# Writing out the three middle batches of a looped attention as straight programs on every engine

## The chip, the cores and the metric

The kernel runs on one core of a Trainium2 chip. The metric is the device time of one launch in microseconds, given as the median of three runs. All traces are of one profiled execution on that core.

## The reference

Input `x` has 4 batches of 256 tokens with 256 features. Three layers follow each other, each behind a layer norm without weights:

```python
x = x + 0.5 * ffn(layernorm(x), router_weight, w_in, w_out, bias)
x = x + attn(layernorm(x), w_q, w_k, w_v, w_o, b_o)
x = x + 0.5 * ffn(layernorm(x), router_weight, w_in, w_out, bias)
```

`ffn` is a mixture of 8 experts, of which each token uses the best two: `silu(a) * b @ w_out.T` with `a, b` the halves of `h = x @ w_in.T`, weighted by a softmax over the two router logits. `attn` is causal attention with 16 heads of 16 features: `q @ k.T / sqrt(256)`, softmax, times `v`, and a projection with `w_o` and a bias. All is in float32.

## The kernel before

TensorE (PE), VectorE (DVE), ScalarE (ACT), GpSimd (POOL) and the queue of SyncE each run a program of their own, and they meet only in semaphores. Products of float32 are taken with a high and a low part, so that most products are three matmuls. The order of the work on each engine is written out by hand.

The first and the last layer, `ffn(0)` and `ffn(1)`, go through 23 blocks of 128 gathered tokens. Seven of them are written out, the next fourteen lie in a loop on a register, the last two are written out again.

The attention, which is what the change touches, is a sweep over batches. `step(b, old, new)` issues eight steps `s` for batch `b`. In the steps 0 and 1 the pairs of heads 6 and 7 of the batch before (`old`) are scored, in the steps 2 to 7 the pairs 0 to 5 of the new batch; a pair goes through the engines with a lag of one step for each stage:

- PE, in every step: `scores` with the tail (the second 128 queries against 256 keys: three matmuls of 512 columns at L1553, a mask at L1554), `turn_probs` (six transposes at L1564, of the pair two steps back), `scores` with the head (three of 256 columns and a mask), `weigh` (18 small matmuls at L1579 to L1581, of the pair three steps back). The steps 0 and 3 also have a `chunk` of queries and keys (eight matmuls at L1520), step 6 has `turn_context` (L1593), step 7 begins with `project_out` (L1600).
- DVE: the maxima of the tail (L1174) and of the head (L1178), the low half of the turned probabilities (`low`, L1187, two for each pair); at the start of step 5 `add_up`, which sums the context of the old batch (L1195) and inverts the row sums (L1197); at the end of step 7 `add_attention` (L1202).
- ACT: the exponentials of tail and head (L792, L800), the high half of the turned probabilities (`high`, L810, two), two copies for each chunk (L778, L779), and in step 6 the copy of the turned context (L818).
- POOL: `mask_keys`, four multiplications (L607) that make `k_head` for the next tail; in step 6 also `divide` (L381).

Four waits set the order around step 5. `weigh` in step 5 overwrites the banks 5 and 6, and waits for both sums of `add_up` (`ctx_summed`). `turn_probs` waits until `low` has read the banks 3 and 4 (`pT_lo_ready`). `project_out` waits for the copy at L818 (`ctxT_ready`). The `chunk` of step 0 waits for `add_attention` of the batch before (`attn_added`), since both use bank 7.

`sweep` is called once by each of PE, DVE, ACT and POOL. It issues `step(0, False, True)` and `step(4, True, False)` as straight code and the batches 1 to 3 in `Fori`, a loop of the engine's sequencer, with `b` in a register. In the loop each wait compares a semaphore with a value computed from `b`, and operands such as `v[:, bass.ds(b * 2 + kt, 1), h, :]` in `weigh`, `xnT[:, k, bass.ds(b * SEQ, SEQ)]` in `chunk` and `row_sum[:, bass.ds(batch, 1), ...]` in the exponentials get their address from a register.

Of the kernel before, what the change touches and what calls it, by code (L numbers as in the profile page):

```python
# [23 lines left out]
BATCH, SEQ, D = 4, 256, 256  # L24
# [55 lines left out]
def build(nc, x_in, wq_in, wk_in, wv_in, wo_in, bo_in, wr_in, win_in, wout_in, bias_in, out):  # L80
    with ExitStack() as ctx:
# [283 lines left out]
        def sweep(eng, step):  # L365

            step(0, False, True)
            with eng.Fori(1, BATCH) as b:
                step(b, True, True)
            step(BATCH, True, False)  # L370

# [92 lines left out]
        def _(pool):  # L464
# [146 lines left out]
            def step(b, old, new):  # L611
                for s in steps_of(new):
# [4 lines left out]
                    if not old and s == BIAS_STEP:  # L617
                        add_bias(1, bo, TPAIRS - 2, 2)

            sweep(pool, step)  # L620
            inverse_root(2, 0, TPAIRS - 1)
            inverse_root(2, TPAIRS - 1)
# [4 lines left out]
        def _(act):  # L627
# [220 lines left out]
            def finish():  # L848
# [6 lines left out]
                turn_out(2, (2,))  # L855

            sweep(act, step)
            finish()
            ffn(1)
# [4 lines left out]
        def _(dve):  # L864
# [402 lines left out]
            def finish():  # L1267
# [22 lines left out]
                choose(0, best_at)  # L1290

            sweep(dve, step)
            finish()
            ffn(1)
# [418 lines left out]
```

How the kernel before makes its waits and increments, by code:

```python
        def reach(eng, signal, count):  # L360
            if not isinstance(count, int) or count > 0:
                eng.wait_ge(signal, count)
# [12 lines left out]
        def divide(eng, b):  # L376
            eng.wait_ge(inv_ready, b)
            eng.wait_ge(ctx_summed, b * 2)
            for qt in range(2):
                ins = eng.tensor_tensor(ctxv[:, qt, :, :], ctxv[:, qt, :, :],
                                        bc(inv_sum[:, qt, :], 2, [P, HEADS, HD]), ALU.mult)
            ins.then_inc(ctx_ready, 1)
# [11 lines left out]
        @block.sync  # L395
# [9 lines left out]
            def pass_on_w_out():  # L405
                for e in range(E):
                    sp.wait_ge(wout_loaded[e], 32)
                    sp.sem_inc(wout_ready)
# [1 line left out]
            def load_w_in(e):  # L411
                sp.dma_start(w_raw[:, e, :, :], win_in[e].rearrange("(k p) n -> p k n", p=P)).then_inc(win_loaded[e], 16)
            for e in range(EARLY):
                load_w_in(e)
            load_w_out(0)
            load_w_out(1)
            load_w_in(EARLY)
            for parity in range(2):
                sp.wait_ge(gathered[parity], 16)
            load_w_out(2)
            for e in range(EARLY + 1, E):
                load_w_in(e)
                load_w_out(e - 1)
                sp.wait_ge(win_loaded[e - 1], 16)
            load_w_out(E - 1)
            for dst, src in ((bias_row, bias_in), (bo, bo_in)):
                sp.dma_start(dst[:, :], src.partition_broadcast(P)).then_inc(bias_loaded, 16)
```

## Time and profile before

| | us |
|---|---|
| median of 3 runs | 427.62 |
| lowest, highest | 424.95, 428.53 |
| the profiled execution's own time | 428.08 |
| its span, from the first to the last instruction | 426.1 |
| PE busy in the span | 401.9 |

The profiled execution lies 0.46 us above the median, and 2.0 us of its time lie outside of its span. The first attention batch is issued up to 186.6 us of the span, the looped batches run from there to 268.6 us, and `ffn(1)` begins to route its tokens at about 288 us.

### The profile page before, as it was taken

Reading aid. Unit: us, or ns where it says so; the run is one execution under the profiler, and the core shown is the slowest. Engines: PE = TensorE matmul, PEld = TensorE weight load, DVE = VectorE, ACT = ScalarE, POOL = GpSimd, SP = SyncE. Lnnn points to the kernel's source line nnn. Section 1 sums busy time; section 2 is a strip of 40 time slices with the busy share of each in tenths; the row PEclk is TensorE's granted clock in tenths of the full one; section 3 lists DMA queues with packets and bytes.
Section 4 is the critical chain, followed back from the end, with each engine's and each line's share of the span. In section 5 each row is a group of like instructions: output and inputs, shape, how many; then the busy total and the mean of one; then the engine's idle time right before and its main releaser. Section 6 shows DMA issues by size and latency. Waiting matters only on the chain.

```text
span 426.1 us, 10185 instructions
## 1 busy us (share of the span) xinstructions
PE 401.9 (94%) x2910; PEld 331.0 (78%) x2911; DVE 299.2 (70%) x620; ACT 257.6 (60%) x640; POOL 237.9 (56%) x307
## 2 busy tenths in 40 slices
PE   8879999999999989699999999988899999999996
PEld 4548888888888857488888888774588888888885
DVE  6777999565665796777678677888255775656666
ACT  2837875566555454788787788732365556555553
POOL 5156445565567269557767679210555555755860
PEclk9889999999999999989999999998999999999999
DMA  7949921112121710000000000007641211112126
GB/s 256 392 121 397 374 70 60 51 42 69 49 49 37 260 50 0 1 2 2 4 1 0 0 0 0 0 2 255 223 141 51 54 60 49 62 49 49 49 87 233
DMA packets 20746, 38.90 MB, mean 91 GB/s; under 512 B 2928, under 2 KB 14448, under 8 KB 20464
## 3 DMA queue, kind: packets, MB, share of 16 engines
q1 hardware_dynamic: 15888, 24.41, 16.4%
q0 software_dynamic: 4544, 12.07, 9.3%
q10 hardware_dynamic: 288, 2.10, 1.3%
q8 instruction: 14, 0.23, 0.2%
q14 instruction: 12, 0.10, 0.1%
HBM read 29.37 MB, written 9.19 MB: 91 GB/s over the span
## 4 chain that ended last, share of the span: by engine, by line
PE 74%; DVE 13%; issue 4%; DMA 3%; ACT 2%; POOL 1%; DVEq 0%; ACTq 0%; POOLq 0%; SPq 0%
PE bank L1381 28%; PE bank L1403 14%; PE bank L1553 7%; PE bank L1391 4%; PE bank L1564 4%; PE bank L1302 3%; PE bank L1520 3%; PE bank L1357 2%; DMA arena<-xn_scratch,gather_row 2%; DVE pT_lo L1187 1%; PE bank L1554 1%; DVE v L1257 1%; PE bank L1600 1%; PE bank L1323 1%; DVE w_lo L904 1%
## 5 line engine op out<-in xcount | busy, mean ns | idle before, releaser
L526 POOL DMA_INDIRECT arena<-xn_scratch,gather_row x46 | 49.3, 1071 | 70.7 <-PE bank L1357 48.2
L532 POOL DMA_INDIRECT y_scratch<-arena,scatter_row x42 | 62.4, 1486 | 37.4 <-ACT arena L695 35.6
L1381 PE MATMUL bank<-w_hi,xT_hi 128*128 x184 | 62.4, 420 | 0.0
L1032 DVE TENSOR_TENSOR wo_lo<-w_out,wo_hi 128x1024 fp32r<-128x1024 f32 x46 | 56.3, 1224 | 3.6 <-PE bank L1403 2.0
L1037 DVE TENSOR_TENSOR gT_lo<-bank,gT_hi 128x512 fp32r<-128x512 f32 x46 | 31.7, 690 | 38.3 <-ACT gT_hi L669 38.3
L1381 PE MATMUL bank<-w_hi,xT_lo 128*128 x184 | 58.0, 396 | 0.0
L1381 PE MATMUL bank<-w_lo,xT_hi 128*128 x184 | 57.7, 395 | 0.0
L662 ACT ACTIVATE arena<-bank 128x512 f32<-128x512 f32 x46 | 27.6, 599 | 47.0 <-PE bank L1381 47.0
L607 POOL TENSOR_TENSOR k_head<-k_hi,head_mask 128x256 fp32r<-128x256 f32 x64 | 38.7, 625 | 29.1 <-PE bank L1554 22.2
L684 ACT ACTIVATE wo_hi<-w_out 128x1024 fp32r x46 | 48.8, 1060 | 5.6 <-issue 3.5
L1021 DVE TENSOR_TENSOR xT_lo<-bank,xT_hi 128x256 fp32r<-128x256 f32 x46 | 19.5, 425 | 36.4 <-ACT xT_hi L654 36.4
L1553 PE MATMUL bank<-k_head,xT_hi 128*128 128x256 f32 (+1 forms) x128 | 40.3, 396 | 1.9 <-ACT probs L800 1.2
L1381 PEld LDWEIGHTS bank<-w_lo,xT_hi 128*128 128x128 f32 x184 | 34.8, 189 | 8.2
L1381 PEld LDWEIGHTS bank<-w_hi,xT_lo 128*128 128x128 f32 x184 | 34.8, 189 | 8.0
L607 POOL TENSOR_TENSOR k_head<-k_lo,head_mask 128x256 fp32r<-128x256 f32 x64 | 38.2, 618 | 0.6 <-DVE k_lo L1161 0.6
L695 ACT ACTIVATE arena<-bank 128x256 f32<-128x256 f32 x42 | 16.2, 386 | 36.9 <-PE bank L1403 36.9
L792 ACT ACTIVATE probs<-bank,neg_max 128x256 f32<-128x256 f32 x64 | 29.9, 479 | 8.9 <-DVE neg_max L1174 8.9
L810 ACT ACTIVATE pT_hi<-bank 128x384 f16<-128x384 f32 x64 | 28.1, 488 | 11.7 <-PE bank L1564 11.0
L1403 PE MATMUL bank<-wo_hi,gT_hi 128*128 128x256 f32 x184 | 33.0, 301 | 1.4 <-ACT gT_hi L669 1.4
L1302 PE MATMUL bank<-ones 128*128 128x512 f16 x94 | 29.2, 447 | 3.9 <-POOL ident L476 1.8
L1187 DVE SCALAR_TENSOR_TENSOR pT_lo<-bank,pT_hi 128x384 f16<-128x384 f32 x64 | 32.4, 549 | 0.5
L1046 DVE TENSOR_TENSOR arena<-arena,bank 128x512 f32<-128x512 f32 x46 | 31.2, 679 | 1.0 <-PE bank L1381 0.9
(194 smaller groups left out, 958.0 us busy)
## 6 DMA issues: line engine op xcount, KB each, us to landing
w_raw<-in_win_t SPq DMA_DIRECT2D x8, 1024.0 KB, 10.3
w_out<-in_wout_t SPq DMA_DIRECT2D x16, 512.0 KB, 7.9
w_out<-y_scratch SPq DMA_DIRECT2D x8, 512.0 KB, 5.7
xn_scratch<-arena ACTq DMA_DIRECT2D x2, 1024.0 KB, 6.5
x<-in_x SPq DMA_DIRECT2D x4, 256.0 KB, 3.4
out<-x SPq DMA_DIRECT2D x4, 256.0 KB, 2.2
arena<-xn_scratch,gather_row POOLq DMA_INDIRECT x46, 3.4
y_scratch<-arena,scatter_row POOLq DMA_INDIRECT x46
```

The lines of the kernel that those rows point to most:

```text
L526: pool.indirect_dma_start(out=xb[j % 2][:, :], out_offset=None, in_=xn_dram, in_offset=bass.IndirectOffsetOnAxis(ap=gather_row[:, j:j + 1] ...
L532: pool.indirect_dma_start(out=y_dram, in_=y[j % 2][:, :], in_offset=None, out_offset=bass.IndirectOffsetOnAxis(ap=scatter_row[:, j:j + 1], ...
L607: ins = pool.tensor_tensor(k_head[s % KSLOTS][:, part, hh, :], k[:, c, :].bitcast(F32), head_mask[:, h % HPC:h % HPC + 1].to_broadcast([P, ...
L684: act.activation(wo_hi[u][:, :, :], w_out[:, bass.ds(e, 1), :, :].rearrange("p o c d -> p (o c) d"), ACT.Copy)\
L1032: dve.tensor_tensor(wo_lo[:, :, :], w_out[:, bass.ds(e, 1), :, :].rearrange("p o c d -> p (o c) d"), wo_hi[u][:, :, :].bitcast(F32), ALU.s ...
L1037: dve.tensor_tensor(gT_lo[:, :, :], bank[4][:, :].rearrange("p (c t) -> p c t", c=HK), gT_hi[:, :, :].bitcast(F32), ALU.subtract).then_inc ...
L1046: dve.tensor_tensor(g[:, :], sa[:, :], bank[2 + u][:, :], ALU.mult).then_inc(g_done, 1)
L1187: dve.scalar_tensor_tensor(pT_lo[u][:, :, :], bank[3 + hh][:, 0:3 * P].rearrange("p (k t) -> p k t", k=3), P_SCALE, pT_hi[u][:, :, :], ALU ...
L1302: pe.matmul(bank[into][:, :], ones[:, :], bc(ones[:, :], 1, [P, 512 // P, P]), start=True, stop=True)
L1381: last = pe.matmul(bank[2 * half + u][:, :], tok[u][:, k, :], wts[:, bass.ds(e, 1), k, half * H:(half + 1) * H], start=(part == 0 and k == ...
L1403: last = pe.matmul(bank[y_bank(j)][:, 0:D], tok[:, c, :], wts[:, c, :], start=(part == 0 and c == 0), stop=(part == 2 and c == HK - 1))
L1553: pe.matmul(to, q[:, 1 if tail else 0, :], keys[:, part, :, 0:width], start=(n == 0), stop=False)
```

## The change

The loop becomes a loop of Python, so that the batches 1, 2 and 3 are issued with numbers in place of registers, one behind the other, in each engine's program. What is computed, in which order, in which tiles and behind which semaphores stays the same. `sweep` is the only function that is edited, and its four callers are those named above.

```diff
         def sweep(eng, step):
 
             step(0, False, True)
-            with eng.Fori(1, BATCH) as b:
+            for b in range(1, BATCH):
                 step(b, True, True)
             step(BATCH, True, False)
```

## Rows read from the trace of the kernel before

**Rows 1.** The page: share of the span in the chain that ended last, by engine.
```profile
PE 74%; DVE 13%; issue 4%; DMA 3%; ACT 2%; POOL 1%; DVEq 0%; ACTq 0%; POOLq 0%; SPq 0%
```

**Rows 2.** Windows, first two looped batches: stretch, us, busy by engine, clock, DMA share, GB/s.
```profile
186.60:214.00 27.40, 27.08 (x292) 22.73 (x289) 19.31 (x41) 22.14 (x87) 19.99 (x35) 1.00 0.01 2
214.00:241.40 27.40, 27.17 (x285) 22.61 (x285) 19.48 (x41) 22.10 (x87) 19.75 (x35) 1.00 0.00 0
```

**Rows 3.** Timeline of PE, the tail scores that open a step: start, length, instruction.
```profile
193.49 0.72 PE L1553 MATMUL bank<-k_head,xT_hi 128*128 128x512 f32 x2
...
196.22 0.72 PE L1553 MATMUL bank<-k_head,xT_hi 128*128 128x512 f32 x2
...
200.45 0.70 PE L1553 MATMUL bank<-k_head,xT_hi 128*128 128x512 f32 x2
...
202.91 0.18 PE L1581 MATMUL bank<-v,pT_lo 128*128 x1
202.95 0.72 PE L1553 MATMUL bank<-k_head,xT_hi 128*128 128x512 f32 x2
...
206.63 0.72 PE L1553 MATMUL bank<-k_head,xT_hi 128*128 128x512 f32 x2 [0.18 <-issue]
...
248.32 0.71 PE L1553 MATMUL bank<-k_head,xT_hi 128*128 128x512 f32 x2
...
251.08 0.73 PE L1553 MATMUL bank<-k_head,xT_hi 128*128 128x512 f32 x2
```

**Rows 4.** Waits in the looped batches, 186.6 to 268.6: total, times, longest.
```profile
PEld bank L1553 <- issue: 0.7, 3, 0.3
```

**Rows 5.** Timeline, all engines, steps 5 to 7 of the first looped batch.
```profile
203.95 1.28 DVE L1195 TENSOR_REDUCE ctxv<-bank 128x256 f32<-128x512 f32 x2
205.37 0.19 PE L1579 MATMUL bank<-v,pT_hi 128*128 x1
205.41 0.63 DVE L1174 TENSOR_REDUCE neg_max<-bank 128x2 f32<-128x512 f32 x1
206.24 0.47 ACT L792 ACTIVATE probs<-bank,neg_max 128x256 f32<-128x256 f32 x1 [0.90 <-DVE neg_max L1174]
206.28 1.01 DVE L1187 SCALAR_TENSOR_TENSOR pT_lo<-bank,pT_hi 128x384 f16<-128x384 f32 x2
206.28 0.18 PE L1581 MATMUL bank<-v,pT_lo 128*128 x1
...
208.16 0.87 ACT L810 ACTIVATE pT_hi<-bank 128x384 f16<-128x384 f32 x2 [0.20 <-PE bank L1564]
...
208.92 0.60 ACT L818 ACTIVATE wv<-bank 128x512 f32<-128x512 f32 x1
...
209.58 1.99 PE L1600 MATMUL bank<-wo,wv 128*128 128x256 f32 x8
```

**Rows 6.** Timeline of the straight first batch: one `weigh`; a maximum and its exponential.
```profile
178.25 0.19 PE L1579 MATMUL bank<-v,pT_hi 128*128 128x32 bf16 x1 [0.32 <-DVE v_rest L1250]
...
178.68 0.18 PE L1581 MATMUL bank<-v,pT_lo 128*128 128x32 bf16 x1
...
179.57 0.68 DVE L1174 TENSOR_REDUCE neg_max<-bank 128x2 f32<-128x512 f32 x1
...
180.29 0.47 ACT L792 ACTIVATE probs<-bank,neg_max 128x256 f32<-128x256 f32 x1 [0.89 <-DVE neg_max L1174]
```

**Rows 7.** Timeline around the first back edge of the loop, PE and DVE.
```profile
213.79 0.18 PE L1581 MATMUL bank<-v,pT_lo 128*128 x1
213.97 0.49 PE L1553 MATMUL bank<-k_head,xT_hi 128*128 128x512 f32 x1
...
214.83 0.68 DVE L1202 TENSOR_TENSOR x<-x,bank 128x512 f32 x1
...
215.67 0.69 PE L1520 MATMUL bank<-arena,wq 128*128 x2
```

**Rows 8.** The page: the queue that brought instructions: packets, MB, share of 16 engines.
```profile
q8 instruction: 14, 0.23, 0.2%
```

## The prediction

> **What bounds the kernel now.** I read the page first. PE is busy for 401.9 of 426.1 us and makes up 74% of the chain that ended last; "issue", time in which an engine waited for nothing that the profile shows, is 4% of it [rows 1]. So an edit of the sequencers' work can pay only where PE stands still or runs below its own pace. The windows of the looped batches come next. The three take 82.0 us together, and the first two 27.4 us each, with PE busy for 27.1 to 27.2 us and its granted clock at 1.00, the level of 2.4 GHz. ACT has 22.1 us of work in a batch, POOL 19.9 and DVE 19.4 [rows 2]. A busy PE isn't a PE at its pace, so the timeline has to say more. Each step opens with the tail scores of a pair, and from one such start to the next is the length of the step. Step 4 takes 202.95 - 200.45 = 2.50 us, with its matmuls one behind the other [rows 3]; I take that as PE's own time for a step without extras. Step 2 has the same work and takes 2.73 us in the first looped batch and 2.76 in the third. Step 5 has it too, and takes 206.63 - 202.95 = 3.68 us [rows 3]. These steps are where something can be won: 0.25 us three times, and 1.18 us three times.
>
> **Step 2.** No wait for another engine shows at this place in the timeline, and `k_head` has been written before. What is left is the sequencer: in the loop it has to compute the value of every wait and the address of every `v` operand, and it falls behind after the slow matmuls of the chunk no longer give it a lead. The straight program has no such instructions. I take the whole excess, 3 x 0.25 = 0.75 us. The bounds are 0 (something else holds the step) and 0.8.
>
> **Step 5.** DVE adds up the old context from 203.95 to 205.23, and PE's `weigh`, which waits for it, begins at 205.37. Its 18 matmuls then start over 0.91 us, and 0.35 us go by from the last start to the tail of step 6 [rows 3, 5]. The same 18 in the straight first batch, behind a wait as well, start over 178.68 - 178.25 = 0.43 us [rows 6]. Between a step's last small matmul and the next tail a dense stretch shows 202.95 - 202.91 = 0.04 [rows 3]. So 0.48 + 0.31 = 0.79 us of this place is work of PE's sequencer; its pause before the tail occurs three times in the looped batches, once in each [rows 4]. The other 0.39 us are the wait for DVE, and stay.
>
> The 0.79 us don't all come through. What is late next is DVE, which is busy without a break from 203.95 on: sums, inverse, two maxima, two `low`, a row that the head scores of step 4 started and not `weigh`. Its second `low` ends at 206.28 + 1.01 = 207.29, and `turn_probs` of step 6 can't overtake it: 0.14 us of signal, as between the sums and `weigh`, make 207.43. Behind it comes ACT: its exponential starts 0.20 us after DVE's maximum has ended (205.41 + 0.63 = 206.04 to 206.24) [rows 5], while in the straight batch it starts 0.04 us after (179.57 + 0.68 = 180.25 to 180.29) [rows 6]. The straight program takes 0.16 us out here. ACT's exponentials of this step, which now end 0.20 us before `high` starts, at 207.96, would end at 207.80. `high` then no longer waits for its `turn_probs`, whose first half DVE releases 0.5 us before the second, and starts at 207.84 in place of 208.16. So the copy of the turned context starts at 208.60 in place of 208.92 and ends at 209.20, and `project_out`, which now starts at 209.58, 0.06 us behind that copy's end [rows 5], starts at 209.26. That is 0.32 us for each batch, 0.96 in all. The least is ACT's shorter start alone, 3 x 0.16 = 0.5 us; the most is all that PE's sequencer takes, 3 x 0.79 = 2.4 us.
>
> **The loop's edges.** At a back edge PE starts its next tail 213.97 - 213.79 = 0.18 us after the last small matmul, 0.14 more than elsewhere; there are two. I cost what it gives back at nothing. The chunk behind it waits for `add_attention` on DVE, which ends at 214.83 + 0.68 = 215.51, and starts at 215.67 [rows 7]. DVE's chain to it begins with the head scores of step 7, ahead of the edge. If that cover were gone, 2 x 0.14 = 0.3 us would come. On DVE, ACT and POOL the edge falls into step 7's idle time, while PE projects.
>
> The page "Runtime: NRT & Kernel Launch" of the Trainium skill says under "Instruction fetch mechanics" that a taken branch whose target isn't in the buffered window forces a fetch before the engine goes on. By that rule each back edge of an engine would hold a fetch. The trace doesn't show it: 0.18 us and no bytes.
>
> **More code.** The straight program fetches the batches 2 and 3, which the loop does not: DMA moved 2 GB/s in the first looped batch and 0 in the second [rows 2]. The first batch fetched its code and was as long as the second, 27.4 us, so I cost this at nothing. What hides it is that the transfer runs ahead of the engines. The same page says that such sequential fetching is hidden since instructions are issued more slowly than they arrive; by it the sum is unchanged.
>
> **The sum.** 0.75 + 0.96 = 1.7 us. The profiled execution's 428.08 us become 426.4. It stood 0.46 above the median of 427.62, so the median becomes 425.9, which is 0.4% less. A measurement of this kernel can tell about 1%, 4.3 us, from no change.
>
> **Rivals.** *More comes back.* All that the looped batches lose against PE's own pace is 3 x 1.18 + 0.75 + 0.3 at the edges + some 0.4 of waiting for `add_attention`, 5.0 us, and the time would be 422.6. It takes a DVE that starts its sums earlier by its own shorter waits. For it speaks that ACT's start shrinks by 0.16 in straight code; against it that DVE's instructions in step 5 already overlap end to start.
>
> *The gain is hidden anyway.* ACT has 22.1 us for eight steps [rows 2], 2.8 us for each with the chunks' copies counted in, no less than PE needs for a plain step; if its pace in step 2 or POOL's `k_head` is what holds the step, PE only waits in another place. Then 0 to 0.5 us come, and the time is 427.4.
>
> *Slower: fetches are exposed.* The first looped batch brought 2 GB/s over 27.4 us, some 55 KB, and the straight program brings that twice more, 110 KB. A packet of the instruction queue has 0.23 MB / 14 = 16 KB and took 426.1 x 16 x 0.002 / 14 = 0.97 us [rows 8]. Seven of them, each holding an engine on the path once, cost 6.5 us; less the 1.7 won, the time is 432.4. It decides from the point where an engine uses up its code faster than a block arrives. PE's share of a batch is some 290 matmuls and as many weight loads in 27.4 us, and each block comes in about 1 us, so only a fetch that is started late could hold it. The first looped batch speaks against it.
>
> **Chances.** The forecast 0.60. More comes back 0.15, of which two thirds pass 1%. Hidden anyway 0.16. Fetches exposed 0.07, of which 0.05 pass 1%. The last 0.02 is for something unnamed, slower or faster. So faster by over 1% 0.11, within 1% 0.83, slower 0.06. The range takes in the first rival nearly whole and the second with the spread of the three runs above the median: 422.6 to 428.7. The forecast's own range is 424.4 to 427.1, from the bounds of its terms.
>
> **What would show it.** In the trace of the changed kernel step 2 takes 2.5 us in all three batches, the 18 matmuls of `weigh` in step 5 start over 0.43 us, still after the second sum on DVE, and the tail follows within 0.05. ACT's exponential starts 0.04 us after the maximum. `project_out` comes 0.3 us sooner behind the head scores of step 4. The chunk of step 0 still waits for L1202. The three batches together take 80.3 us in place of 82.0, with 1 to 2 GB/s in each. The stages behind are as long as before. The prediction is wrong if a gap without a releaser opens at some place in the straight batches, if step 5 shrinks by more than 0.5 us, or if a stage behind the attention changes its length by more than 1 us.

## The result

The changed kernel takes 424.68 us in the median of 20 runs (422.21 to 426.25), against 427.54 for the kernel before in runs beside it (20 runs, 424.92 to 430.25). The ratio is 0.9938, with a 95% interval of 0.9916 to 0.9960: 2.65 us less, 1.7 to 3.6 by the interval. The forecast was 1.7 us less.

The page of the changed kernel, its first line, the share of the ending chain by engine, and the queue that brings instructions:

```profile
span 421.8 us, 9602 instructions
...
q8 instruction: 19, 0.31, 0.3%
...
PE 71%; DVE 16%; DMA 6%; issue 3%; POOL 2%; ACT 2%; POOLq 0%; DVEq 0%; ACTq 0%; SPq 0%
```

583 instructions are gone from the 10185 of before, branches and arithmetic on registers, and "issue" has fallen from 4% to 3% of the chain [rows 1]. The queue q8 brought 19 packets in place of 14 [rows 8], and a second one, q14, brought 16 in place of 12 by the two pages.

The windows of the three middle batches (stretch, length, busy time by engine, granted clock, DMA share, GB/s) answer to [rows 2]:

```profile
183.90:210.40 26.50, 26.25 (x290) 21.90 (x287) 18.99 (x40) 21.83 (x86) 19.77 (x35) 1.00 0.01 2
210.40:237.10 26.70, 26.44 (x290) 21.91 (x287) 19.39 (x41) 21.98 (x86) 19.76 (x35) 1.00 0.01 2
237.10:263.80 26.70, 26.43 (x290) 21.91 (x287) 19.39 (x41) 21.98 (x86) 19.76 (x35) 1.00 0.01 2
```

They are 26.5, 26.7 and 26.7 us long. Each now fetches its own code at 2 GB/s, and each is shorter than the looped ones. The granted clock is 1.00, as before.

To see where in a batch the time went I took the start of every step from the timeline of PE in both traces, as in [rows 3], and subtracted neighbours. All step lengths below are made so, in us:

```
step             0     1     2     3     4     5     6     7
before, batch 1  4.26  2.60  2.73  4.23  2.50  3.68  4.59  2.75
after,  batch 1  4.26  2.50  2.54  4.26  2.50  2.81  5.03  2.60
before, batch 2  4.45  2.49  2.78  4.23  2.48  3.64  4.59  2.74
after,  batch 2  4.51  2.48  2.54  4.26  2.48  2.82  5.03  2.59
before, batch 3  4.47  2.48  2.76  4.23  2.49  3.64  4.58  2.60
after,  batch 3  4.51  2.48  2.54  4.26  2.48  2.82  5.03  2.60
```

From the tail scores that open batch 1 to those that open the fifth batch is 81.99 us before and 79.93 after, 2.06 us less. Step 2 gives 0.65 of it, the steps 5 and 6 together 1.18, the pairs of step 7 and the step 0 behind it 0.20, step 1 of the first batch 0.10; step 3 takes back 0.09.

The timeline of the changed kernel at steps 2 and 5 to 7 of its batch 1, and at the place where the loop had its edge. It answers to [rows 3], [rows 5] and [rows 7]:

```profile
190.69 0.71 PE L1553 MATMUL bank<-k_head,xT_hi 128*128 128x512 f32 x2
...
193.23 0.70 PE L1553 MATMUL bank<-k_head,xT_hi 128*128 128x512 f32 x2
...
201.00 1.28 DVE L1195 TENSOR_REDUCE ctxv<-bank 128x256 f32<-128x512 f32 x2
...
202.34 0.19 PE L1579 MATMUL bank<-v,pT_hi 128*128 128x32 bf16 x1
...
202.46 0.63 DVE L1174 TENSOR_REDUCE neg_max<-bank 128x2 f32<-128x512 f32 x1
...
202.78 0.18 PE L1581 MATMUL bank<-v,pT_lo 128*128 128x32 bf16 x1
...
202.80 0.71 PE L1553 MATMUL bank<-k_head,xT_hi 128*128 128x512 f32 x2
203.12 0.48 ACT L792 ACTIVATE probs<-bank,neg_max 128x256 f32<-128x256 f32 x1 [0.84 <-DVE neg_max L1174]
203.32 1.01 DVE L1187 SCALAR_TENSOR_TENSOR pT_lo<-bank,pT_hi 128x384 f16<-128x384 f32 x2
204.02 0.98 PE L1564 MATMUL bank<-ident,probs 128*128 128x128 f32 x6
...
205.48 0.61 ACT L818 ACTIVATE wv<-bank 128x512 f32<-128x512 f32 x1
...
206.21 1.97 PE L1600 MATMUL bank<-wo,wv 128*128 128x256 f32 x8
...
211.44 0.68 DVE L1202 TENSOR_TENSOR x<-x,bank 128x512 f32<-128x512 f32 x1
212.17 0.70 PE L1520 MATMUL bank<-arena,wq 128*128 128x256 f32 x2
```

The 18 small matmuls of step 5 start over 202.78 - 202.34 = 0.44 us in place of 0.91, and the tail of step 6 follows 0.02 us behind the last start in place of 0.35. `weigh` begins 0.06 us after the second sum (202.28), where it took 0.14. ACT's exponential starts 0.03 us after DVE's maximum (203.09), where it took 0.20. Step 5 is still 0.3 us over a plain step, and step 6 has become longer: `turn_probs` there starts at 204.02, 0.14 us behind the first of the two `low` (203.88), and its second half waits for the second. PE now gets there before DVE does. The waits of this stretch, 183.9 to 263.9, say the same by name (engine, what waits, for whom: total, times, longest):

```profile
PEld bank L1564 <- issue: 1.4, 6, 0.3
PEld bank L1579 <- DVE ctxv L1195: 0.9, 3, 0.3
...
PEld bank L1520 <- DVE x L1202: 0.4, 2, 0.2
PE bank L1564 <- DVE pT_lo L1187: 0.3, 2, 0.2
```

Before, the pause behind the small matmuls bore the name "issue" [rows 4]; that row is gone, and in its place stand the sums, `add_attention` and `low`, all on DVE. The new row of "issue" at L1564 is the same wait for `low`: it stands six times for the two halves of `turn_probs` in the three steps 6 (0.31 and 0.16 us each), where PE's sequencer waits for L1187 in an instruction of its own (203.91 and 204.38), and the weight loads' idle time is then put down to no engine.

**The spans differ by more than the batches.** 426.1 - 421.8 = 4.3 us, of which the three batches are 2.06. The rest lies in code that the change leaves alone. The first attention batch took 1.0 us less in its steps 6 and 7 (4.38 + 2.55 against 5.19 + 2.73). The windows of the same 2.4 to 3 us there, before and after:

```profile
181.00:184.00 3.00, 2.81 (x29) 2.68 (x29) 2.16 (x7) 2.76 (x12) 0.24 (x1) 0.50 0.03 5
```

```profile
179.00:181.40 2.40, 1.92 (x29) 1.62 (x29) 2.34 (x6) 2.35 (x11) 0.22 (x1) 1.00 0.03 7
```

After a pause of PE of 1.4 us, in which it waits for DVE in both kernels, the granted clock was 0.50 in the one, the level of 1.2 GHz, and 1.00 in the other. Everything ahead of that batch's second tail (164.47 us before, 162.76 after) ran 1.71 us sooner, and what lies behind the fifth batch's first tail was 0.5 us longer. Whether these belong to the change is a question for a second profile of each kernel, below.

### The profile page after: what moved, and what is told of

The parts are those of the page before. It is cut to its first block, busy times and chain, and to the rows that moved or that the text cites. A ratio compares the mean times of both kernels' runs of the same rounds, so it can differ in the third digit from the quotient of the medians.

```text
span 421.8 us, 9602 instructions
## 1 busy us (share of the span) xinstructions
PE 397.2 (94%) x2910; PEld 326.7 (77%) x2911; DVE 299.0 (71%) x620; ACT 257.2 (61%) x640; POOL 237.8 (56%) x307
## 4 chain that ended last, share of the span: by engine, by line
PE 71%; DVE 16%; DMA 6%; issue 3%; POOL 2%; ACT 2%; POOLq 0%; DVEq 0%; ACTq 0%; SPq 0%
PE bank L1381 28%; PE bank L1403 14%; PE bank L1553 6%; PE bank L1391 4%; PE bank L1564 4%; PE bank L1520 3%; PE bank L1357 2%; DMA w_out<-y_scratch 2%; DVE pT_lo L1187 2%; DMA arena<-xn_scratch,gather_row 2%; DVE x L1071 2%; DMA y_scratch<-arena,scatter_row 1%; DVE arena L890 1%; DVE neg_max L1174 1%; DVE v L1257 1%
## 5 line engine op out<-in xcount | busy, mean ns | idle before, releaser
L1403 PE MATMUL bank<-wo_hi,gT_hi 128*128 128x256 f32 x184 | 33.0, 301 | 1.4 <-ACT gT_hi L669 1.4
L1187 DVE SCALAR_TENSOR_TENSOR pT_lo<-bank,pT_hi 128x384 f16<-128x384 f32 x64 | 32.4, 548 | 0.6 <-ACT pT_hi L810 0.6
L1302 PE MATMUL bank<-ones 128*128 128x512 f16 x94 | 27.4, 426 | 4.8 <-POOL ident L476 1.8
```

What stands on the lines that cost most here:

```text
L1187: dve.scalar_tensor_tensor(pT_lo[u][:, :, :], bank[3 + hh][:, 0:3 * P].rearrange("p (k t) -> p k t", k=3), P_SCALE, pT_hi[u][:, :, :], ALU ...
L1403: last = pe.matmul(bank[y_bank(j)][:, 0:D], tok[:, c, :], wts[:, c, :], start=(part == 0 and c == 0), stop=(part == 2 and c == HK - 1))
```

## The experiments

The theory, A: what the change removes is work of PE's sequencer, and next to it ACT's and PE's late start behind a wait; the loop's edges and the fetching of code cost little. The rivals are named in the expectations as B (spread over the engines), C (DVE's and ACT's waits), D (edges and fetching), E (more code costs), F (PE's own pace), G (writing out pays everywhere) and H.

As a whole kernel's time varies by some 4 us from run to run, the verdicts rest on the step lengths, which agree within 0.03 us almost everywhere between profiles of the same program (the granted clock over the three batches was 1.00 in all 14 profiles); the ratio is given where it was measured, always against the kernel before.

**Which engine's loop matters.** Three kernels write out the loop on some engines and keep it on the others:

```diff
-            with eng.Fori(1, BATCH) as b:
-                step(b, True, True)
+            if eng is nc.tensor:              # also: nc.scalar; both of them
+                for b in range(1, BATCH):
+                    step(b, True, True)
+            else:
+                with eng.Fori(1, BATCH) as b:
+                    step(b, True, True)
```

PE alone:

> Only PE is written out; DVE, ACT and POOL keep the loop. Measure: the three middle batches, from the tail scores that open the first to those that open the fifth batch, 82.0 us before and 79.9 after. Theory A (PE's sequencer work is what the change removes, ACT's late start behind DVE adds a little): step 2 of each batch falls to 2.5 us, the 18 small matmuls of step 5 start over 0.43 us, ACT's exponential still starts 0.20 us after the maximum. The three batches take 80.3 to 80.5 us, the kernel 1.5 us less than before. Rival B (every engine's registers cost, and the gain is spread evenly): 81.3 us. Rival C (DVE's and ACT's waits hold steps 5 and 6, so PE alone gives only step 2): 81.2 us, with steps 5 and 6 together still 8.2 us.

ACT alone:

> Only ACT is written out. Theory A: ACT's exponential starts 0.03 us after the maximum, but its copy of the first turned probabilities waits for PE, so the three batches stay at 81.9 to 82.0 us. Rival B (spread evenly): 81.3 us. Rival C (ACT's start is what holds steps 5 and 6): 3 x 0.16 less, 81.5 us, with steps 5 and 6 together at 8.05 us.

PE and ACT:

> PE and ACT are written out, DVE and POOL keep the loop. Theory A: all of the gain is here, the three batches take 79.9 to 80.1 us and steps 5 and 6 together 7.85 us. Rival B (spread evenly): 80.9 us.

Measured, three batches and ratio with its interval: PE alone 80.47 us, 0.9962 (0.9943 to 0.9981); ACT alone 81.68 us, 0.9991 (0.9964 to 1.0019); both 79.96 us, 0.9977 (0.9952 to 1.0002). So PE has 1.52 of the 2.06 us, ACT behind it another 0.51, and DVE and POOL 0.03. B falls, since the shares are uneven and two engines have none. C falls: with PE alone the steps 5 and 6 take 7.96 us in place of 8.27. What ACT adds shows in step 6, 5.15 us with PE alone and 5.03 with both, and in step 2, 2.59 and 2.54. In the timeline of the kernel with PE alone, ACT's exponential starts 0.21 us after DVE's maximum ends (204.10 + 0.62 = 204.72):

```profile
204.10 0.62 DVE L1178 TENSOR_REDUCE neg_max<-bank 128x2 f32<-128x512 f32 x1
```

```profile
204.93 0.47 ACT L796 ACTIVATE probs<-bank,neg_max 128x256 f32<-128x256 f32 x1 [0.93 <-DVE neg_max L1178]
```

With ACT alone written out it starts 0.03 us after (202.97 to 203.00), and yet the steps 5 and 6 take 8.24, 8.21 and 8.20 us, 0.02 to 0.03 less than with the loop: ACT's copy waits for PE there, as theory A had it. The three batches together gained 0.31 us, where I had expected at most 0.1; most of it lies in the steps 1 and 2, and I didn't follow it up.

**Addresses or waits.** This one keeps the loop on every engine and takes only the register out of the address of `v`, so that every batch is weighed with the values of batch 0:

```diff
-                        rows = v[:, bass.ds(b * 2 + (kt - 2 * ago), 1), h, :]
+                        rows = v[:, kt:kt + 1, h, :]
```

> The loop stays on all engines, but weigh reads the values of batch 0 in every batch, at a fixed address (so the context of the batches 1 to 3 is computed from other values); its waits keep their registers. It parts the addresses from the waits. Theory A1 (the addresses are most of PE's sequencer work): the 18 small matmuls of step 5 start over 0.43 to 0.55 us and step 2 takes 2.5 us; the three batches take 80.4 to 80.8 us. Rival A2 (the waits are most of it): the 18 matmuls still pause, over 0.8 us or more, and the three batches take 81.7 to 82.0 us.

The three batches took 80.68 us: 1.31 us of the 1.52 that PE's part is worth came from one operand's address. The small matmuls of step 5, in the timeline of PE:

```profile
203.38 0.19 PE L1579 MATMUL bank<-v,pT_hi 128*128 128x32 bf16 x1
...
203.82 0.18 PE L1581 MATMUL bank<-v,pT_lo 128*128 128x32 bf16 x1
203.84 0.71 PE L1553 MATMUL bank<-k_head,xT_hi 128*128 128x512 f32 x2
```

They start over 0.44 us. The first of them also comes sooner behind DVE's sums, 0.06 us (202.04 + 1.28 = 203.32 to 203.38) in place of 0.14, although its wait still compares with a register:

```profile
202.04 1.28 DVE L1195 TENSOR_REDUCE ctxv<-bank 128x256 f32<-128x512 f32 x2
```

So PE's late start at this place, too, belongs to the computed address. The steps 2, 5 and 6 have the lengths that they have with PE written out (2.59, 2.81 and 5.15 us in both, within 0.01), though all waits of PE still compare with a register. The profile counts 10185 - 9993 = 192 instructions less, 64 for each batch, 8 for each `weigh`; so a `weigh` held 8 register instructions more, and without a lead they cost 0.91 - 0.44 = 0.47 us, 0.06 us each. What is left between this kernel and PE written out, 0.21 us, is in step 7 (2.83 and 2.74 against 2.59 and 2.60), less what step 0 behind it gives back: the two back edges.

**Registers without an edge.** The middle batches inside of a loop with a single trip:

```diff
-            with eng.Fori(1, BATCH) as b:
-                step(b, True, True)
+            with eng.Fori(0, 1) as i:
+                for b in range(1, BATCH):
+                    step(i + b, True, True)
```

> All three middle batches are written out inside of a loop that runs once: registers in all waits and addresses, no back edge, and as much code as in the changed kernel. Theory A (registers are the cost): 81.7 to 82.0 us for the three batches, only the two back edges' pause of 0.14 us gone and most of it taken by the wait for add_attention; step 2 still 2.75 us, step 5 still 3.65 us. Rival D (the loop's edges and its fetching are the cost): 79.9 us as in the changed kernel. Rival E (more code costs time, hidden in the changed kernel's gain): over 82.3 us.

Three batches 79.92 us, ratio 0.9953 (0.9929 to 0.9976). This is the number of rival D, but the experiment can't speak for it: the profile counts 9614 instructions, 12 more than the changed kernel and 571 fewer than the looped one, so a loop that runs once had its register turned into numbers. It shows that an empty loop frame costs nothing here, and it is a second reading of the changed kernel. That the addresses are the cost rests on the run before it.

**The edge and its cover.** In the kernel before, DVE's `add_attention` goes from the end of step 7 to its beginning, where DVE waits for PE in any case:

```diff
+                    if old and s == OUT_STEP + 1:
+                        add_attention(b)
                     if old if s < SLAG else new:
                         maxima(b, s, True)
...
                     if s == OUT_STEP + 1:
-                        if old:
-                            add_attention(b)
-                        else:
+                        if not old:
```

> The kernel before with one move: DVE's add_attention goes from the end of step 7 to its beginning, where DVE is idle, so that the chunk of step 0 in the batches 2 and 3 no longer waits for it. It tests the cover of the loop's edges. Theory A (the back edge's pause of 0.14 us in step 7 and the chunk's wait in step 0 lie one behind the other, and the wait swallows what the edge costs): step 7 still takes 2.74 us in the batches 1 and 2, step 0 falls from 4.46 to 4.26 us in the batches 2 and 3, and the three batches take 81.6 us. Rival H (the chunk is late for another reason): step 0 stays at 4.46.

Step 0 fell to 4.23 and 4.24 us in the batches 2 and 3, step 7 stayed at 2.77 and 2.74, the three batches took 81.52 us. So the edge's 0.14 us and the chunk's wait of 0.2 us do lie one behind the other, and the wait is one for `add_attention`. Rival H falls. But the cover isn't whole: written out, a step 7 with its step 0 went from 7.20 and 7.21 us to 7.11 and 7.10. In [rows 7] the chunk starts 0.16 us after `add_attention`, in the changed kernel 0.05 us after (211.44 + 0.68 = 212.12 to 212.17). The edge itself is swallowed; it is PE's quicker start behind the wait that gives 0.1 us each time. With only the address of `v` fixed the chunk's own addresses are still computed, and there it starts 0.16 us behind (213.29 to 213.45).

**DVE's row after the change.** The inverse of the row sums (L1197) goes from step 5, between the sums and the maxima, to step 3, where DVE is idle. Once in the kernel before and once in the changed one:

```diff
             def add_up(b):
...
-                dve.reciprocal(inv_sum[:, :, :], sums).then_inc(inv_ready, 1)
+            def invert(b):
+                sums = row_sum[:, bass.ds(b - 1, 1), :, :].rearrange("p o q h -> p (o q) h")
+                dve.reciprocal(inv_sum[:, :, :], sums).then_inc(inv_ready, 1)
...
                     if s in CHUNK_STEP and (old if s < SLAG + 2 else new):
                         low(b, s)
+                    if old and new and s == CHUNK_STEP[1]:
+                        invert(b)
```

> The kernel before with one move: DVE inverts the row sums in step 3, where it is idle, in place of step 5 between the sums and the maxima (0.26 us of DVE's row). Theory A (DVE's row and ACT behind it bound the steps 5 and 6 with the loop too): ACT's chain starts 0.26 us sooner, but turn_probs behind PE's slow weigh holds the copies, so 0 to 0.2 us for each batch: 81.4 to 82.0 us. Rival F (PE's sequencer alone is the bound there): 82.0 us.

> The changed kernel with the same move of the inverse to step 3. Theory A (what is late in steps 5 and 6 after the change is DVE's row: turn_probs of step 6 behind the second low): everything behind starts 0.26 us sooner in each batch, steps 5 and 6 together take 7.55 to 7.65 us in place of 7.85, the three batches 79.1 to 79.3 us, and the kernel is 0.8 us faster than the changed one. Rival F (PE is at its own pace there): 79.9 us, steps 5 and 6 together 7.85 us.

In the looped kernel nothing moved: 81.97 us, the steps 5 and 6 together 8.26, 8.22 and 8.20, ratio 1.0005 (0.9983 to 1.0027). In the changed kernel they took 7.65 us in place of 7.85, and the three batches 79.32 in place of 79.93. The same edit is worth 0 with the loop and 0.61 us without it, so before the change PE's sequencer held the place and after it DVE's row does. F falls for the changed kernel. The size is less than the 0.8 us expected, since DVE's `low` came 0.20 us sooner behind the head scores of step 4 and not 0.26. The whole kernel had a ratio of 0.9978 (0.9952 to 1.0004), which can't be told from that of the changed one.

**Writing out where PE has a lead.** The loops over the expert blocks in both ffn layers, on PE, ACT and DVE, are written out as well:

```diff
-                with pe.Fori(0, LOOPED) as i:
+                for i in range(LOOPED):
```

> The changed kernel with the loops over 14 expert blocks written out too, on PE, ACT and DVE, in both ffn layers. Theory A (registers cost only where an engine's sequencer has no lead; the blocks' PE has slow matmuls of 0.4 us and the written-out blocks take 4.86 us like the looped ones): 0 us, within 0.5 us of the changed kernel. Rival G (writing out pays everywhere): 28 blocks x 0.1 us or more, 3 us less. Rival E (more code costs time): over 1 us more than the changed kernel.

A block takes 4.86 us in both kernels, within 0.03 on every one of the 28 places, read off the starts of its first L1403 matmul, and the queue brought 26 packets in place of 19. So G falls, and no block pays for its fetches. The whole kernel had a ratio of 0.9992 (0.9973 to 1.0011), 2.3 us above that of the changed one, which was measured beside other runs of the kernel before. The two intervals don't overlap, and by its mark (over 1 us more) rival E holds for the kernel as a whole. Where the profiled execution lost its time can be seen. Its first block's matmul L1403 starts at 37.4 us, where the other 13 profiles have it at 33.6 to 35.7, and what parts them is mostly the granted clock. The windows from 26 to 36 us in the changed kernel, in the kernel before and in this one, with that matmul at 33.9, 35.7 and 37.4:

```profile
26.00:36.00 10.00, 9.64 (x53) 7.85 (x54) 7.58 (x11) 5.27 (x10) 6.37 (x7) 1.00 0.70 218
```

```profile
26.00:36.00 10.00, 9.43 (x41) 7.32 (x42) 6.66 (x8) 5.11 (x9) 5.24 (x6) 0.83 0.71 231
```

```profile
26.00:36.00 10.00, 9.14 (x31) 6.74 (x32) 5.51 (x7) 4.31 (x7) 4.26 (x6) 0.66 0.72 234
```

All 14 profiles fall in this order: 1.00 in six of them, with the matmul at 33.6 to 33.9; 0.83 to 0.85 in seven, with 34.9 to 35.7; 0.66 in this one alone. ACT's first copy L654 is late too, at 27.64 in place of 26.4 to 27.2, since ACT splits `w_in` ahead of it (L647) and the load that this waits for came 0.5 us later than in any other profile. As only one of its ten executions has a trace, it stays open whether the longer code costs something ahead of the blocks; the blocks themselves don't show it.

**Second profiles.** Both kernels once more, unchanged:

> The kernel before once more, for a second profile. The three middle batches take 82.0 us again, within 0.05. In the first batch, which no kernel of this study changes, the steps 6 and 7 took 5.19 and 2.73 us in the profile of before at a granted clock of 0.50 for part of it, and 4.38 and 2.55 in that of the changed kernel. If this difference is one of executions and not of the change, it can be absent here; if it belongs to the kernel before, it is here again.

> The changed kernel once more, for a second profile: 79.9 us for the three middle batches, within 0.05, every step as before.

The three batches took 82.00 and 79.95 us, against 81.99 and 79.93 in the first profiles. In the first attention batch the steps 6 and 7 took 5.15 + 2.86 us in the kernel before and 5.08 + 2.93 in the changed one. The fall of the clock is now in both, and it shows in 7 of all 14 profiles, with and without the change. So 1.0 us of the 4.3 between the first two spans was luck. So were the 1.7 us ahead of that batch: they are there in full at the first combine matmul (L1403) of `ffn(0)`, at 35.65 us before and 33.91 in the changed kernel, with granted clocks of 0.83 and 1.00 from 26 to 36 us, and in the second profiles it is the other way round, 33.82 us at 1.00 before and 35.11 at 0.83 after. The second pair of spans is 423.9 and 423.9 us, with the batches 2.05 us apart all the same: the rest of the kernel, up to the first attention batch above all, varies by as much as the change is worth.

**Both moves on the changed kernel:**

> The changed kernel with both moves on DVE: the inverse of the row sums in step 3 and add_attention at the beginning of step 7. Theory A: step 0 falls from 4.51 to 4.26 us in the batches 2 and 3, steps 5 and 6 together stay at 7.65 as with the first move alone; the three batches take 78.8 us in place of 79.9 and the kernel is 1.1 us faster than the changed one, 3.2 us or 0.75% faster than the one before. Rival H: 79.3 us, as with the first move alone.

The three batches took 78.87 us, step 0 4.26 us in all three, the steps 5 and 6 together 7.65, and the kernel 422.15 us with a ratio of 0.9889 (0.9857 to 0.9920): 4.7 us less than before, where the batches account for 3.1; where the other 1.6 come from isn't shown. The chunk of step 0 in its timeline, PE and DVE:

```profile
208.31 0.69 DVE L1204 TENSOR_TENSOR x<-x,bank 128x512 f32<-128x512 f32 x1 [0.91 <-PE bank L1604]
...
210.51 0.70 PE L1557 MATMUL bank<-k_head,xT_hi 128*128 128x512 f32 x2
...
212.12 1.03 PE L1524 MATMUL bank<-arena,wq 128*128 128x256 f32 x4
```

`add_attention` is over at 209.00, three microseconds before the chunk needs its bank. This is the fastest version of the study, and the only one whose ratio lies below that of the changed kernel; their intervals overlap by 0.0004.

## Why the prediction was right

**The place and the sum.** The 1.7 us forecast were to come from the three middle batches, and 2.06 did; the measured 2.65 has these 2.06 inside of its interval, 1.7 to 3.6, and the 1.7 of the forecast at its lower edge. The stages behind the middle batches kept their length within 0.5 us.

**Step 2** was put at 0.75 us and gave 0.65. It falls to 2.54 and not to 2.50, since PE now waits a little for DVE's `low`. That PE's sequencer is most of the reason is shown by the kernel with a fixed address of `v`, 2.59 us, as with PE alone written out; the last 0.05 us of each come only with ACT. The prediction named the values of the waits and the addresses together; only the addresses have a price on PE in these steps.

**Steps 5 and 6** were put at 0.32 us a batch and gave 0.43, 0.38 and 0.37. The parts of the argument hold in the trace: the small matmuls over 0.44 us, the sums' wait staying, `turn_probs` 0.14 to 0.15 us behind the second `low`, ACT 0.03 us behind the maximum. What was mis-sized is the hand-over on ACT. I let `high` start 0.04 us after the recorded end of the exponentials; it starts 0.12 us before that end, as the last one ends at 204.84:

```profile
204.63 0.21 ACT L800 ACTIVATION_READ_ACCUMULATOR probs<-bank,neg_max 128x1 f32 x1
204.72 0.88 ACT L810 ACTIVATE pT_hi<-bank 128x384 f16<-128x384 f32 x2
```

Counted from the start of DVE's sums the copy therefore ends 0.48 us sooner than with the loop (5.09 in place of 5.57) and not 0.32. Of this 0.06 us don't come through, since now PE's own row ends last: `project_out`, which I had at the end of ACT's copy, is at 206.21 just behind `weigh`, with the copy over at 206.09. What is left is 0.42 us in this batch.

**A sign that came.** The prediction called itself wrong if step 5 shrank by more than 0.5 us. It shrank by 0.82 to 0.86, from 3.68, 3.64 and 3.64 us to 2.81 or 2.82, and step 6 grew by 0.44. The sign contradicts the prediction's own working, in which 0.79 us leave step 5 and come back in part as a wait in step 6; the forecast of 0.32 us is one for the two steps together. So it speaks against the way that the sign was set and not against the mechanism.

**The edges** were costed at nothing and gave 0.20 us. The cover that I named is there, as moving `add_attention` shows; what I left out is that PE starts sooner behind this wait, after 0.05 us in place of 0.16.

**More code** was costed at nothing. Each straight batch fetched at 2 GB/s and was as short as its neighbours. What the page "Runtime: NRT & Kernel Launch" of the Trainium skill says under "Instruction fetch mechanics", that sequential fetching is hidden, agrees with this. Its rule that a taken branch forces a fetch where the target has left the window had nothing to act on here: the looped batches 2 and 3 moved no bytes, and no gain of that kind came back.

**The rivals.** *More comes back* didn't happen: of the 5.0 us lost against PE's own pace 2.06 came, and DVE's row, which moving the inverse shows to be the bound, holds part of the rest. *Hidden anyway* and *fetches exposed* have no trace. *ACT's pace* has a small part in step 2, 0.05 us of each batch's 0.2: it didn't hide the gain, and it came back with ACT written out. In the price of *fetches exposed*, seven packets of 0.97 us are 6.8 us and not 6.5, so that rival's time should have been 432.7.

## What to carry to other kernels

A loop on registers costs where many short instructions with computed addresses follow a wait that has used up the sequencer's lead, and next to nothing where matmuls of 0.4 us stand between them: look for starts that pause inside of a group which elsewhere is dense, and take out that one operand's register before writing out the whole loop. After such a change the same wait points to the next engine; an edit that was worth nothing before can be worth something now, as the moved inverse was here. Where a whole kernel varies by more than the change is worth, compare the stretches between two marks of the program in both traces, and look at the granted clock in those where the spans part.

## What the runs showed of the hardware

Behind DVE's release ACT starts after 0.03 us in the straight program and after 0.20 to 0.21 in the looped one. In the kernel with ACT alone written out, ACT starts after 0.03 us and PE after 0.14 (200.88 + 1.28 = 202.16 to 202.30), both behind a looped DVE, so it goes with the waiting engine and not with the releasing one. PE starts `weigh` after 0.06 us where its addresses are numbers, even with a wait on a register, and after 0.14 where they are computed; the chunk has 0.05 and 0.16. That isn't one price for all waits: `turn_probs` starts 0.14 us behind `low` in the changed kernel too, where PE's sequencer waits in an instruction of its own. For ACT no run parts the address from the wait.

A back edge of the loop cost PE 0.14 us and no transfer.

In the first attention batch PE pauses for 1.4 us behind DVE. In 7 of 14 executions of that code PE had the 1.2 GHz level for some 3 us from about the end of this pause (0.2 us before it to 0.4 behind it), and in the others not at all, at a price of 1.0 to 1.2 us. A pause of 1.2 us some 9 us earlier was followed by no such fall in any of the 14. At the first gathered blocks of `ffn(0)`, behind PE's wait for the weights and tokens, a fall is there in 8 of 14 executions. The first combine matmul comes 1 to 2 us later with it, and 3.5 us in the one execution where it lasted longer.
